# First mixture's experts: weight rows stream under stationary tokens, the bias enters as a one-hot product, and the activations are turned as f16

## What is computed

```python
h = einsum('td,efd->etf', xt, fc1_w) + fc1_b[:, None, :]   # 256 -> 512 columns
xh, g = h[..., :256], h[..., 256:]
a = gelu(g) * xh * geglu_mult[:, None, :]
yexp = einsum('etf,edf->etd', a, fc2_w) + fc2_b[:, None, :] # 256 -> 256 columns
y = einsum('etd,te->td', yexp, comb)                        # comb: weights of the 3 picked experts
```

## Time and profile before

| | |
|---|---|
| median of 3 runs | 1495.68 us (1491.24 to 1498.45) |
| profiled execution | 1503.98 us, span 1502.2 us |
| mean granted TensorE clock | 0.848 |
| TensorE matmul busy | 1071.6 us (71%) |
| VectorE busy | 1050.2 us (70%) |
| ScalarE busy | 723.5 us (48%) |
| GpSimd busy | 503.5 us (34%) |
| first transpose of m0x | 403.91 us |
| last output of m0x | 583.22 us |

### The profile page before, as it was taken

One profiled execution on the slowest core, in us unless ns is written; L12 is line 12 of the kernel. 1 busy time (PEld: TensorE's weight loads), 2 busy tenths in 40 slices (PEclk: granted clock), 3 DMA queues, 4 the chain that ended last, 5 costly groups with the idle time before them and its releaser, 6 DMA issues. The chain is left out here.

```text
span 1502.2 us, 31497 instructions
## 1 busy us (share of the span) xinstructions
PE 1071.6 (71%) x9872; PEld 748.8 (50%) x9872; DVE 1050.2 (70%) x2316; ACT 723.5 (48%) x1444; POOL 503.5 (34%) x644
## 2 busy tenths in 40 slices
PE   4637788774299998577666977266579996379991
PEld 2222233224288875354444764144456664378881
DVE  3968999987555554565986764778758886745553
ACT  4666555553265543224445742144358886234440
POOL 0063777762254553731001100000026665232204
PEclk9558999995599999887888979689769997589996
DMA  6600000001344544312000000000023331112214
GB/s 196 231 12 1 0 1 1 0 1 50 99 122 138 157 131 154 95 43 85 0 1 0 1 1 1 0 1 0 0 72 113 111 112 52 50 55 64 64 50 122
DMA packets 47766, 89.68 MB, mean 60 GB/s; under 512 B 8352, under 2 KB 34629, under 8 KB 46789
## 3 DMA queue, kind: packets, MB, share of 16 engines
q1 hardware_dynamic: 40578, 67.98, 14.7%
q0 software_dynamic: 6912, 18.88, 4.5%
q10 hardware_dynamic: 144, 1.05, 0.2%
HBM read 71.84 MB, written 16.04 MB: 59 GB/s over the span
## 5 line engine op out<-in xcount | busy, mean ns | idle before, releaser
L1190 POOL TENSOR_TENSOR scan_ch<-scan_hs,scan_ct 128x452 f32<-128x452 f32 x128 | 143.4, 1141 | 75.1 <-DVE scan_hs L1300 51.3
L1213 PE MATMUL scan_py<-scan_ch,ident 128*128 128x452 f32 x256 | 131.7, 605 | 40.8 <-POOL scan_ch L1190 31.3
L1300 DVE TENSOR_TENSOR_SCAN scan_hs<-scan_abar,scan_bx 128x452 f32<-128x452 f32 x128 | 133.2, 1084 | 0.5 <-ACT scan_abar L1262 0.3
L458 PE MATMUL m0x_ph<-m0x_xb,m_w_hi 128*128 128x128 f16 x456 | 99.9, 221 | 1.2 <-ACT m0x_xb L1962 1.0
L459 PE MATMUL m0x_ph<-m0x_xb,m_w_hi 128*128 128x128 f16 x456 | 99.9, 221 | 0.0
L460 PE MATMUL m0x_ph<-m0x_xb,m_w_lo 128*128 128x128 f16 x456 | 99.6, 220 | 0.0
L2027 DVE TENSOR_SCALAR m3x_a<-m3x_ph,m3x_b 128x128 f32<-128x128 f32 x184 | 49.6, 342 | 70.0 <-ACT m3x_ah L1988 70.0
L1213 PEld LDWEIGHTS scan_py<-scan_ch,ident 128*128 128x128 f32 x256 | 41.1, 194 | 111.3 <-POOL scan_ch L1190 100.7
L1262 ACT ACTIVATE scan_abar<-ssm_dt,ssm_a 128x448 f32<-128x448 f32 x128 | 80.9, 640 | 22.9 <-DVE scan_hs L1300 21.6
L2024 DVE SCALAR_TENSOR_TENSOR m0x_a<-m0x_ph,m0x_b,m0x_gate 128x128 f32<-128x128 f32 x114 | 34.7, 346 | 72.4 <-issue 36.7
L1988 ACT ACTIVATE m3x_ah<-m3x_ph,m3x_b 128x128 f16<-128x128 f32 x184 | 50.3, 386 | 65.7 <-PE m3x_ph L460 61.7
(11 more groups left out here) (691 smaller groups left out, 3822.9 us busy)
## 6 DMA issues: line engine op xcount, KB each, us to landing
mha_wbuf<-m3w SPq DMA_DIRECT2D x32, 512.0 KB, 3.7
tok_wbuf<-m0w SPq DMA_DIRECT2D x15, 768.0 KB, 5.4
m0x_b<-m0b SPq DMA_DIRECT2D x57, 128.0 KB
m_out<-m0x_yo SPq DMA_DIRECT2D x57, 128.0 KB
m3x_b<-m3b SPq DMA_DIRECT2D x23, 128.0 KB, 3.0
m_out<-m3x_yo SPq DMA_DIRECT2D x23, 128.0 KB
m_rows<-m0r_parts SPq DMA_DIRECT2D x4, 448.0 KB
m_rows<-m3r_parts SPq DMA_DIRECT2D x4, 448.0 KB
```

The lines of the kernel that those rows point to most:

```text
L458: pe.matmul(out, w_hi, x_hi, start=start, stop=False)
L1190: pool.tensor_tensor(ch[r][:], hs[r][:], ct[n % 2][:], ALU.mult).then_inc(weighed, 1)
L1213: pe.matmul(py[c][:, 0:GT], core.ident[:], ch[u % R][:], start=n == 0, stop=n == NS - 1).then_inc(summed, 1)
L1300: dve.tensor_tensor_scan(hs[u % R][:], abar[c][:, 0:GT], bx[u % R][:], 0.0, ALU.mult, ALU.add).then_inc(scanned, 1)
```

## The change

A function of its own, `stage_gated_experts`, takes the first mixture. The tokens of a block become stationary and the expert's whole row of 512 hidden columns moves, 2 chunks x 3 products = 6 matmuls. The bias is a seventh matmul of 512 columns: `m.b1` holds all experts' biases as rows, f16 high halves in partitions 0 to 14 and low rests in 32 to 46, and the stationary operand is one column of the one-hot matrix `sel`, repeated 128 times. The result has tokens on partitions, so GELU and the product are one instruction each over 128x256. High half and low rest are made in that shape, and four f16 transposes (`flip`) turn them into `pf`, from which ScalarE copies them into `flat` (128x512, `take_flat`); `second` reads `flat`.

Around it: GpSimd no longer copies biases and its loop, like SP's, is written out; the biases are loaded as 128x512 f32 and scaled and split on VectorE in the token stage; GpSimd makes `sel` there; `s1` shares the buffer of `w_fc`, whose load moves from SP ahead of the loop to ScalarE's queue at step 12.

```diff
-        self.bg.load(sp, 0)
...
+        if n == 12:
+            act.wait_ge(self.s1.lo_done, 2)
+            self.bg.load(act, 0)
...
-            dve.tensor_scalar(m.b1[:, :, 0:m.NF // 2], m.b1[:, :, 0:m.NF // 2], WS, None,
-                              ALU.mult).then_inc(self.ready, 1)
+            dve.tensor_scalar(m.b1[:], self.b1[:], WS, None, ALU.mult).then_inc(self.ready, 1)
...
+        if m.gelu:
+            dve.scalar_tensor_tensor(m.b1[32:64], self.b1[32:64], WS, m.b1[32:64], ALU.mult,
+                                     ALU.subtract).then_inc(self.ready, 1)
...
+                def first(n, e):
+                    p = n % 2
+                    pe.wait_ge(xb_ready, n + 1)
+                    need(pe, a_ready, n - 1)
+                    for k in range(KC):
+                        w_hi, w_lo = m.row_of(e, k)
+                        pe.matmul(ph[p][:], xb[p][:, k, :], w_hi, start=k == 0, stop=False)
+                        pe.matmul(ph[p][:], xb[p][:, KC + k, :], w_hi, start=False, stop=False)
+                        pe.matmul(ph[p][:], xb[p][:, k, :], w_lo, start=False, stop=False)
+                    pe.matmul(ph[p][:], m.pick(e), m.b1[:], start=False, stop=True).then_inc(h_ready, 1)
+
+                def flip(n):
+                    pe.wait_ge(hi_ready, n + 1)
+                    pe.wait_ge(lo_ready, n + 1)
+                    need(pe, flat_ready, n)
+                    for part in range(2):
+                        for f in range(FH):
+                            last = pe.transpose(pf[:, 0, part * FH + f, :], parts[n % 2][:, part, f, :], core.ident16[:])
+                    last.then_inc(flipped, 1)
...
+                turn(0)
+                turn(1)
+                e[0] = expert(0)
+                first(0, e[0])
+                e[1] = expert(1)
+                first(1, e[1])
+                turn(2)
+                flip(0)
+                for n in range(N):
+                    if n + 3 < N:
+                        turn(n + 3)
+                    if n + 2 < N:
+                        e[n + 2] = expert(n + 2)
+                        first(n + 2, e[n + 2])
+                    if n + 1 < N:
+                        flip(n + 1)
+                    second(n, e[n])
+                    prepare.on_tensor(pe, n)
...
+            def _(act):
...
+                for n in range(2):
+                    take_tokens(n)
+                for n in range(2):
+                    open_gate(n)
+                    high(n)
+                take_tokens(2)
+                take_flat(0)
+                for n in range(N):
+                    if n + 3 < N:
+                        take_tokens(n + 3)
+                    if n + 2 < N:
+                        open_gate(n + 2)
+                    if n + 1 < N:
+                        take_flat(n + 1)
+                    if n + 2 < N:
+                        high(n + 2)
+                    prepare.on_scalar(act, n)
...
+            def _(dve):
...
+                for n in range(N):
+                    if n + 2 < N:
+                        activate(n + 2)
+                    output(n)
+                    if n + 2 < N:
+                        low(n + 2)
+                    prepare.on_vector(dve, n)
```

More of the change, by code:

```diff
@@ L134, with __init__ @@
 class Split:
-    def __init__(self, st, tag, loads):
+    def __init__(self, st, tag, loads, buf=None):
         self.loads = loads
-        self.buf = [st.sb(f"{tag}_{load[0]}_f32", list(load[1].shape)) for load in loads]
+        self.buf = buf or [st.sb(f"{tag}_{load[0]}_f32", list(load[1].shape)) for load in loads]
         self.landed = [st.sem(f"{tag}_{load[0]}_landed") for load in loads]
-        self.hi_done = st.sem(f"{tag}_hi")
+        self.hi_done, self.lo_done = st.sem(f"{tag}_hi"), st.sem(f"{tag}_lo")
     def load(self, sp):
@@ L153, in low @@
         dve.wait_ge(self.hi_done, n + 1)
-        dve.scalar_tensor_tensor(self.loads[n][3], self.buf[n][:], WS, self.loads[n][2], ALU.mult, ALU.subtract)
+        dve.scalar_tensor_tensor(self.loads[n][3], self.buf[n][:], WS, self.loads[n][2], ALU.mult, ALU.subtract).then_inc(self.lo_done, 1)
 class Ternary:
@@ L301, in __init__ @@
                           lambda dve, out, tot, inv: dve.tensor_scalar(out, tot, inv, 1e-6, ALU.mult, ALU.add), 1)
+        self.s1 = Split(st, "s1", [(f"h{h}", d["s1"][:, h * 1024:(h + 1) * 1024], flat(w.s1_hi)[:, h * 1024:(h + 1) * 1024],
+                                    flat(w.s1_lo)[:, h * 1024:(h + 1) * 1024]) for h in range(2)],
+                        [self.bg.buf[0][:, h * 1024:(h + 1) * 1024] for h in range(2)])
         self.b2_scaled = self.bg.neg[0:1, 0:2 * D].bitcast(F32)
@@ L513, in stage_tokens, with _ @@
         with nc.Block() as block:
+            @block.gpsimd
+            def _(pool):
+                mw.make_sel(pool)
             @block.sync
@@ L1364, in buffers, with row_of, pick @@
         self.out = nc.dram_tensor(f"{self.name}_out", [self.blocks * 128, D], F32, kind="Internal").ap()
+    def row_of(self, e, k):
+        at, n = 2 * k * self.NF * 128, KC * self.NF * 256
+        return [w[:].rearrange("p e k n -> p (e k n)").bitcast(mybir.dt.uint8)[:, bass.ds(e * n + at, 256 * self.NF)].bitcast(F16)
+                for w in (self.w1_hi, self.w1_lo)]
+    def pick(self, e):
+        return self.sel[:].bitcast(mybir.dt.uint8)[:, bass.ds(e * 2, 2)].bitcast(F16).to_broadcast([128, 128])
     def first(self, e, k, f):
@@ L1431, in high, with make_sel @@
         ins.then_inc(self.hi_done[b], 1)
+    def make_sel(self, pool):
+        m, made = self.m, Chain(pool, self.sel_made)
+        made.step(pool.memset(m.sel[:], 0.0))
+        for base in (0, -32):
+            made.step(pool.affine_select(out=m.sel[:], in_=m.sel[:], compare_op=ALU.not_equal, fill=1.0, base=base,
+                                         pattern=[[-1, m.E]], channel_multiplier=1))
     def scale_small(self, dve):
@@ L1963, in take_tokens @@
                                    ACT.Copy).then_inc(xb_ready[p], 1)
[L1965 to L1974, removed]
                 def high(n):
@@ L1992, in _ @@
                 take_tokens(1)
[L1993 to L2001, removed]
+                high(0)
+                take_tokens(2)
+                high(1)
                 for n in range(N):
-                    if m.gelu and n + 1 < N:
-                        high(n + 1)
                     if n + 3 < N:
@@ L2007, in _ @@
                     if n + 2 < N:
-                        take_gate(n + 2) if m.gelu else high(n + 2)
-                    if prepare is not None:
-                        prepare.on_scalar(act, n)
+                        high(n + 2)
             @block.vector
@@ L2048, in _ @@
                 for n in range(-2, N):
-                    if m.gelu and 0 <= n + 1 < N:
-                        low(n + 1)
                     if n + 2 < N:
                         product(n + 2)
-                        if not m.gelu:
-                            low(n + 2)
+                        low(n + 2)
                     if n >= 0:
                         output(n)
-                    if prepare is not None and n >= 0:
-                        prepare.on_vector(dve, n)
             @block.sync
@@ L2079, in _ @@
                 output_bias(At(0, 1))
-                if prepare is not None:
-                    prepare.on_sync(sp)
                 steps(sp, N - 2, step)
@@ L2084, in _ @@
                     store(At(0, n))
-                if prepare is not None:
-                    prepare.at_end(sp)
                 sp.wait_ge(stored[0], 16 * ((N + 1) // 2))
@@ L3377, in by_strip, with twice_in_rows @@
     return out
+def twice_in_rows(b):
+    out = np.zeros((128, b.shape[1]), b.dtype)
+    out[0:b.shape[0]] = out[32:32 + b.shape[0]] = b
+    return out
 def layout(i):
```

164 lines of the change are left out of this document (132 added, 32 removed).

## The result

| | median | range, runs | ratio to before, same chip |
|---|---|---|---|
| before | 1496.99 us | 1491.24 to 1498.45, 4 | |
| after | 1480.97 us | 1478.59 to 1484.32, 4 | 0.9906 [0.9884, 0.9927] |
| after, a second time (run e5) | 1486.02 us | its before 1497.40 | 0.9935 [0.9916, 0.9954] |

By the ratios the change makes the kernel 0.94% faster, 0.65% the second time: 14.1 and 9.7 us, more than the half percent that was forecast as the border to no change. (The medians of the table lie further apart, 16.0 and 11.4 us. A gain on the kernel before is given by the ratio here, a difference of two changed kernels by their medians.) The forecast was 1491.8 us, a gain of 3.85.

What follows compares the result with a forecast made beforehand. TensorE was taken to bound the kernel. Terms of -14.0, +2.7, +3.7, +1.1, +2.0, +0.3 and +0.35 sum to -3.85 us, from a median of 1495.68 to 1491.8 us, range 1482 to 1503.

Steps and rivals of the forecast that it cites:

- the pace: Steady blocks of the m0x stage: 2.68 us each instead of 2.95, -14.0 us over 52 blocks.
- the stops: TensorE waiting in mid-stage: +2.7 us for the w_proj load, +3.7 for w_fc, +1.1 for the two reduces.
- the end: End of the m0x stage: last output hangs on its bias load in both kernels; the flip adds 0.3 us.
- the start: First blocks of the m0x stage: turn(4) 2.3 us later, earlier gathers give back 0.3, so +2.0 us.
- bias load nothing: Loading the bias's repeated-column operand in `first` hides under the matmul before it: 0 us, bounds 0 to 0.1.
- Rival E: Wide matmuls faster than the trace's row: blocks held at 2.40 us by the output-bias loop, 1477 us; chance 0.04.
- Rival D: Loop back to the flip takes over 0.3 us more: TensorE waits every flip, pace 2.85 to 3.0, 1501 us; chance 0.10.
- Turn and `second` keep 0.22 and 0.73: Within each m0x block, the turn stays at 0.22 us and the second layer at 0.73 us.
- The reduces: Reduces of 2.28 us at steps 20 and 37 delay the next product: some 0.6 us each, +1.1 together.
- The absorption argument: With `low(n+2)` behind `output(n)` on VectorE, output waits over some 0.5 us stop TensorE; before, a further block hid them.
- The token stage: ScalarE's first weight work waits for the larger bias scaling: +0.35 us, bounds 0 to 0.74.
- Rival B: Late outputs are absorbed: pace won, loads and reduces cost no more than before, -11.4 us, 1484; chance 0.20.

Runs made afterwards that it cites:

- e5: The changed kernel, unaltered, measured a second time: 1486.02 us, 0.9935 of before.
- e4: The kernel before with expert 0's first-layer weights for every block, so that the weight addresses are constants: 0.9917 of before.
- e7: The changed kernel with each wide row cut into four pieces of 128 columns, 28 matmuls instead of 7: 1.0082 of before.
- e12: The changed kernel with expert 0's first-layer rows and bias for every block, so that those addresses are constants: 0.9946 of before.
- e10: The kernel before with only the w_fc load moved to step 12 and `s1` sharing its buffer: 0.9994 of before.
- e8: The changed kernel with w_fc loaded ahead of the loop on SP again, `s1` in its own buffers, `gate` and `a` single: 0.9914 of before.
- e6: The changed kernel with output biases and stored outputs four buffers deep instead of two, bias loads issued four blocks ahead: 1477.32 us, 0.9871 of before.
- e2: The changed kernel with the low rest of block n+2 ahead of the output of block n on VectorE: 0.9944 of before.
- e11: The kernel before with expert 0's first-layer weights throughout, output biases and output buffers four deep, and w_fc's load moved to step 12: 1458.98 us, 0.976 of before.
- e3: The changed kernel without the seventh wide matmul, leaving the first layer's bias out: 0.9913 of before.

## Why the prediction came out as it did

The direction and the mechanism were right, the size was not: -3.85 us forecast, -14.1 and -9.7 measured, -12.2 in the stage, where the forecast had -14.0 + 7.5 + 2.0 + 0.3 = -4.2. Its likeliest case, less than half a percent either way (0.51), did not come; faster by more had 0.35. The 8.0 us between -4.2 and -12.2 are four terms of the sum: the pace 3.6, the stops 3.5, the end 1.6, and the start 0.7 the other way. What the short matmuls paid beyond their columns the prediction left unnamed; e4, e7 and e12 show that it is the register work of their addresses.

- **TensorE stays the bound, wide matmuls at 0.215 us, flip 0.22, bias load nothing: right.** First is 1.51 us as forecast. Rival E, with the 131 ns of the Trainium skill (TensorE: Matmul & The Clock Gate, section "Back-to-back issue gap"), is refuted by the 215 to 220 ns between starts. Rival D didn't come: in quiet blocks no flip waits, and GELU of 128x256 took 0.38 us where 0.44 was taken.
- **"Turn and `second` keep 0.22 and 0.73": the second was wrong.** It takes 0.66. The pace is 2.61 instead of 2.68, 52 x 0.07 = 3.6 us. The 0.73 was read from one block that was not typical: in before, too, the second takes 0.66 us in the median of the stretch's 52 blocks and 0.73 or more in only 5. From its first matmul at 414.83, shown under e4, to turn(4) at 415.49 it is 0.66. In the block of the earlier trace rows the second matmul starts 0.18 us behind the first at 503.56, where the next ones stand 0.11 apart; why, no run shows:

```profile
503.74 0.27 PE L459 MATMUL m0x_py<-m_w_lo,m0x_ah 128*128 x1
503.85 0.27 PE L460 MATMUL m0x_py<-m_w_hi,m0x_al 128*128 x1
```

- **The stops: mis-sized by 3.5 us.** The forecast added 2.7 + 3.7 + 1.1 = 7.5 to the 3 us of before, "a loss of 3.7, so +2.7" and "+3.7". TensorE stood 6.6 and 5.9 us in after, 3.2 and 1.4 in before: +4.0. The place and the chain were right. But the load of w_fc cost 2.0 to 2.8 us, that of w_proj 1.8 in after and 1.4 in e5; the forecast had 3.7 for each. The wait behind w_fc was 2.88 us, not 4.2, and of it 0.9 was absorbed, not 0.5. The reduces came out about right, 0.4 to 1.1 us each, though the sum had a slip there: 1.05 late less 0.3 spare is 0.75, not 0.6.
- **The absorption argument holds, its remedy doesn't.** e10 against e8 shows the asymmetry: the moved load costs 0 in before and 2.8 us in after. e6 shows that nearly all remaining stops are output biases. But "`low(n+2)` now stands behind `output(n)`" named one victim, and e2 shows that another takes its place.
- **The start: right, +2.7 for +2.0.** From turn(1) to turn(4) it is +2.7 for the +2.3 forecast. The 0.3 that earlier gathers were to give back didn't come: the first turn is 5.9 us behind the cast instead of 8.2, but turn(1) 11.5 to 11.6 in both kernels. turn(4) is late behind first(2), which waits for take_tokens(2), queued behind the gates and high halves; timeline of TensorE of after:

```profile
411.52 0.39 PE L1931 MATMUL m0x_ph<-m_w_hi,m0x_xb 128*128 x1 [1.47 <-ACT m0x_xb L1983]
```

- **The end: -1.3, not +0.3.** SP's written-out loop issues an output bias about 1.1 us after the output's end where the earlier trace rows have 1.38, and behind turn(56) there are less than three blocks left, each 0.3 us shorter. That these two make up the 1.6 us is argued, not shown.
- **The token stage: +0.35 can't be seen.** ScalarE's wait of the earlier trace rows grew from 0.70 to 0.95 us, but the cast at which the m0x stage begins moves by 1.7 us between after and e5 and by 3.2 between the two profiles of before.
- **Rival B (late outputs absorbed, 1484)** is where the time came out, but half of its reason is wrong: the stops did grow by 4 us. B with the true second would be 1484 - 3.6 = 1480.4; e6, in which the late biases are absorbed, measured 1477.3.

**What stays open.** The two comparisons of the same pair of kernels give 14.1 and 9.7 us with intervals that overlap; the stage's 12.2 lies between. Whether the old layout can have cheap addresses and the right expert's weights at once, which e11 prices at (0.9871 - 0.976) x 1496 = 17 us below e6, was not tried. The fourth mixture has little part in the 17: its stage took 162.5 us in e11 and 162.5 to 163.8 in the others. Nor was the kernel before run with nothing but four-deep buffers; its stops of 1.4 to 3.2 us leave little to gain.

**Best version.** e6, the change with output biases four deep: 1477.32 us, 0.9871 of before.

## What to carry to other kernels

A stream of short matmuls whose weight addresses are computed cost more than its columns here, 84 ns instead of 56: run such a stream once with constant addresses to see by how much, before changing its layout. When a loop gets shorter, look at every small load in it, how far ahead it is issued against its slowest landing, and deepen its buffers in the same change. And take the pace of a block from several blocks, a stage's time from two executions: 0.07 us in one row was 3.6 us of the sum, and 7 to 8 us of one stage was chance.

## What the runs showed of the hardware

- 128-column matmuls with a new weight tile each ran 56 ns apart with constant addresses (e4), 84 ns with two register instructions to every three, and once 56 ns with them, right behind matmuls at the half clock (before, 413.49 to 414.83); 512-column ones 215 ns apart with either (after, e12).
- A stationary operand that is one column repeated 128 times added no time that can be seen: 2.61 us with its product, 2.40 without (e3).
- A 128 KB load that SP issued 1.5 us behind ScalarE's 1 MB load landed 6.5 us after its issue; the median of the stage's 57 such loads is 3.3 (after).
